# Second cross attention: one token tile and eight heads a unit, fp32r scores, five blocks of 128 keys

## The reference, cut to what matters

```python
h = _layernorm(x, ln2_w, ln2_b)
q = (h @ q_w + q_b).reshape(B, T, H, HD).transpose(0, 2, 1, 3)      # B, T, H, HD = 2, 1024, 16, 16
k = (enc @ k_w + k_b).reshape(B, S, H, HD).transpose(0, 2, 1, 3)    # S = 77, enc has 192 features
v = (enc @ v_w + v_b).reshape(B, S, H, HD).transpose(0, 2, 1, 3)
attn = jnp.einsum('bhtd,bhsd->bhts', q, k) * scale
attn = jnp.where(enc_mask[:, None, None, :], neg, attn)
attn = jax.nn.softmax(attn, axis=-1)
ca = jnp.einsum('bhts,bhsd->bhtd', attn, v).transpose(0, 2, 1, 3).reshape(B, T, C)
x = x + ca @ out_w + out_b
```

## Time and profile before

| | us |
|---|---|
| median of 3 runs | 1820.11 |
| the runs | 1815.75, 2371.29, 1820.11 |
| the profiled execution | 1816.95 |
| its span | 1815.2 |
| of it, second cross attention (1550.9 to 1678.3) | 127.4 |

### The profile page before, as it was taken

The page is one execution under the profiler, slowest core; times in us unless marked ns, Lnnn a source line. Parts: engine busy times, 40 slices in busy tenths (PEclk is TensorE's granted clock), DMA queues, the critical chain, the costliest instruction groups (busy, mean ns, idle before and its releaser), DMA issues. The chain is left out here.

```text
span 1815.2 us, 28598 instructions
## 1 busy us (share of the span) xinstructions
PE 1657.3 (91%) x9572; PEld 1025.1 (56%) x9572; DVE 1149.9 (63%) x2009; ACT 1067.1 (59%) x1407; POOL 959.6 (53%) x734
## 2 busy tenths in 40 slices
PE   5889999999999999988999889997898988898799
PEld 3334444444444444376666778885444436565579
DVE  4456777776777777385777753346778754776513
ACT  3436888888888888844554533311576763444452
POOL 1236888888888888951222630201334443466405
PEclk9999999999999999999999999997899999999899
DMA  2001211101110111030000010102333321000101
GB/s 91 18 24 36 68 41 48 41 35 41 38 61 35 41 35 36 24 105 27 1 1 1 13 33 24 30 13 49 91 72 96 81 63 42 9 1 1 35 16 47
DMA packets 54161, 70.82 MB, mean 39 GB/s; under 512 B 18160, under 2 KB 41868, under 8 KB 54063
## 3 DMA queue, kind: packets, MB, share of 16 engines
q1 hardware_dynamic: 54063, 69.54, 13.7%
HBM read 41.72 MB, written 2.37 MB: 24 GB/s over the span
## 5 line engine op out<-in xcount | busy, mean ns | idle before, releaser
L1412 POOL TENSOR_TENSOR x<-x,sa_p_buf 128x1024 f32<-128x1024 f32 x190 | 452.2, 2380 | 109.6 <-ACT sa_p_buf L1233 97.2
L1325 DVE TENSOR_REDUCE sa_mx<-sa_front 128x1 f32<-128x512 f32 x512 | 327.5, 681 | 109.1 <-PE sa_front L1126 107.7
L1233 ACT ACTIVATE sa_p_buf<-sa_score 128x1024 f32<-128x1024 f32 x256 | 249.2, 1024 | 115.9 <-PE sa_score L1164 115.9
L1179 PE MATMUL sa_out<-sa_p_buf,sa_v_buf 128*64 128x512 f32 x1024 | 246.2, 602 | 0.0
L607 ACT ACTIVATE sa_p_buf<-sa_score 128x1024 f32<-128x1024 f32 (+1 forms) x160 | 140.6, 943 | 75.0 <-PE sa_score L555 74.9
L402 DVE TENSOR_REDUCE sa_mx<-sa_front 128x1 f32<-128x512 f32 (+1 forms) x224 | 136.5, 651 | 31.4 <-PE sa_front L316 28.0
L2005 POOL TENSOR_TENSOR x<-x,bias_out 128x1024 f32<-128x1024 f32 x24 | 59.6, 2496 | 166.3 <-POOLq L2335 143.3
L1872 POOL TENSOR_TENSOR ca_probs<-ca_s_sb,ca_inv 128x616 f32<-128x616 f32 x64 | 77.9, 1218 | 120.8 <-DVE ca_inv L1787 120.8
L1179 PEld LDWEIGHTS sa_out<-sa_p_buf,sa_v_buf 128*64 128x64 f32 x1024 | 64.9, 136 | 126.9 <-issue 99.1
L1126 PE MATMUL sa_front<-sa_k_hi,sa_q_hi 64*128 64x512 f32 x512 | 116.7, 452 | 19.1 <-DVE sa_mx L1325 15.6
L1243 ACT ACTIVATE sa_score<-sa_m_all 128x1024 f32<-128x1024 f32 x128 | 130.8, 1033 | 1.0 <-DMA sa_m_all<-sa_m_line 0.6
(11 more groups left out here) (241 smaller groups left out, 3482.1 us busy)
## 6 DMA issues: line engine op xcount, KB each, us to landing
sa_v_buf<-o SPq DMA_DIRECT2D x16, 512.0 KB, 5.1
sa_m_all<-sa_m_line SPq DMA_DIRECT2D x16, 512.0 KB, 3.7
x<-sa_m_line SPq DMA_DIRECT2D x16, 512.0 KB, 4.4
x<-in_x SPq DMA_DIRECT2D x8, 512.0 KB, 6.7
sa_q_stack<-sa_hi SPq DMA_DIRECT2D x32, 128.0 KB, 2.6
sa_k_stack<-sa_hi SPq DMA_DIRECT2D x32, 128.0 KB, 2.6
sa_recip<-sa_den_out SPq DMA_DIRECT2D x32, 128.0 KB, 2.7
ff_w<-in_L_xattn_ff_w SPq DMA_DIRECT2D x16, 128.0 KB, 2.2
```

The source lines that it names most:

```text
L1179: mm = pe.matmul(out_ps[64 * j:64 * j + 64, :], v_buf[:, b, kt, 64 * j:64 * j + 64], p_buf[:, s % NPB, j, :], start=(kt == 0), stop=(kt == ...
L1233: nc.scalar.activation(p_buf[:, s % NPB], score_ps[s % len(score_ps)][:], ACT.Exp, scale=SCALE).then_inc(exp_done, G)
L1325: dve.tensor_reduce(mx[:, b, j, qt, half:half + 1], front_ps[bank(item, j)][:], AX.X, ALU.max).then_inc(drained, 1)
L1412: nc.gpsimd.tensor_tensor(acc[:, h], prev, cur, ALU.add).then_inc(added, 1)
```

## The change

A new function `block_attention` takes the place of `cross_attention` for the second block. The first cross attention keeps the old function. In the new one:

- A unit is one tile of 128 tokens and eight heads (one group): 4 chunks, 2 groups, 4 tiles, 32 units. It again has 8 by 77 = 616 scores on a partition.
- Queries and keys are split into an fp32r high part and an fp32r rest. `score` is three products (high by high, high by low, low by high), each two fp32r matmuls of 308 columns: six matmuls. The split query takes one more DVE instruction for four units (`query_low`). The masked keys exist twice: the high ones are made on DVE (`high_keys`), the low ones on POOL (`low_keys`), one each for the four combinations of group and batch.
- The 616 probabilities of a token stand without gaps (padded to 640) and are turned as five blocks of 128 keys: five transposes, an eviction of 640 numbers.
- The values stand in the same order: block by block of 128 key rows, in which a row holds the 16 features of its own head and zeros elsewhere (`v_blk`, ten blocks, made from the context repeated eight times, `ctx_rep`, and a mask `v_own`). `weighted` runs for two units at once: five float32 matmuls of 256 columns, all 128 output partitions.
- The value bias is added on ACT when a chunk's output is stored (`store`, 512 numbers, every fourth slot); DVE's `copy` is gone. `bv` is loaded as two columns in place of a broadcast row.
- POOL clears `ctx_rep` (2,560 numbers a partition) first, then makes `own`, `v_own` (640 numbers: one memset and two selects), clears `probs` (1,280), makes the low keys of the first combination; then the slots begin.

The core of the diff:

```diff
+                def score(n):
+                    i, g, b = n // TQ, group(n), batch(n)
+                    if tile(n) == 0:
+                        pe.wait_ge(q_split, i + 1)
+                        pe.wait_ge(high_set, keys_needed(n))
+                        pe.wait_ge(low_set, keys_needed(n))
+                    if n >= 2:
+                        pe.wait_ge(s_taken, n - 1)
+                    rows = slice(tile(n) * P, (tile(n) + 1) * P)
+                    for part, (qs, ks) in enumerate(((q_hi, keys_hi), (q_hi, keys_lo), (q_lo, keys_hi))):
+                        for h in range(2):
+                            mm = pe.matmul(s_ps[n % 2][:, h, 0:HH * TC], qs[:, i % 2, rows],
+                                           ks[:, g, b, h * HH * TC:(h + 1) * HH * TC], start=(part == 0), stop=(part == 2))
+                def weighted(n):
+                    if not unit(n) or n % PAIR != PAIR - 1:
+                        return
+                    pe.wait_ge(t_done, n + 1)
+                    ...
+                    for blk in range(NBLK):
+                        mm = pe.matmul(o_ps[:, first * P:(tile(n) + 1) * P], v_blk[:, batch(n), blk, group(n), :],
+                                       turned[:, n // PAIR % 2, blk].rearrange("p u t -> p (u t)"),
+                                       start=(blk == 0), stop=(blk == NBLK - 1))
+                def turn(n):
+                    pe.wait_ge(scaled, n + 1)
+                    if n:
+                        pe.wait_ge(t_done, n)
+                    else:
+                        pe.wait_ge(v_set, NV)
+                    for blk in range(NBLK):
+                        mm = pe.transpose(t_cols[:, at], probs[:, n % 2, at], ident[:])
+                def slot(n):                      # PE
+                    score(n)
+                    query(n + Q_AHEAD)
+                    for i in values_in(n):        # blocks 0-3 in slot 0, 4-6 in slot 1, 7-9 in slot 2
+                        values_of(i)
+                    weighted(n - O_LAG)
+                    turn(n - T_LAG)
+                def slot(n):                      # ACT
+                    store(n - C_LAG)
+                    exponent(n - 1)
+                    query(n + Q_AHEAD)
+                    evict(n - T_LAG)
+                def slot(n):                      # DVE
+                    take(n)
+                    query_low(n + Q_AHEAD)
+                    for i in values_in(n):
+                        values_of(i)
+                    if 0 < n < len(MADE):
+                        high_keys(*MADE[n])
+                    invert(n - 1)
+                pool.memset(ctx_rep[:], 0.0).then_inc(padded, 1)
+                own_rows(own[:], own_made, [[-dh, HR]], 0, dh, 1)
+                own_rows(v_own[:], v_own_made, [[P, NBLK], [-TC, HR], [0, dh]], 0, TC, 1)
+                pool.memset(probs[:], 0.0).then_inc(padded, 1)
+                pool.wait_ge(padded, 2)
+                low_keys(*MADE[0])
+                def slot(n):                      # POOL
+                    scale(n - D_LAG)
+                    shift(n)
+                    if n + 1 < len(MADE):
+                        low_keys(*MADE[n + 1])
-                            (bv[:], row(L1["v_b"]).to_broadcast((P, D)), kv_in[1]),
+                            (bv[:], L1["v_b"].rearrange("(g p) -> p g", p=P), kv_in[1]),
-                cross_attention(nc, "ca1", thin, hT, ctxT, ident, kv,
-                                {"key_low": lambda b: ctx_low[:, b, :]},
-                                oT, loads)
+                block_attention(nc, "ca1", hT, ctxT, ident, kv, lambda b: ctx_low[:, b, :], oT, loads)
```

272 lines of the change are left out of this document (271 added, 1 removed).

## The result

| | before | after |
|---|---|---|
| median of 20 runs, us | 1819.16 | 1823.28 |
| profiled span, us | 1815.2 | 1823.2 |
| second cross attention, entry to last store, us | 127.3 | 131.9 |

A forecast was written before the change was run, and what follows sets the result against it. A circuit through PE, DVE and POOL, not PE's work alone, was to bound the rounds; fill +8.0, steady part -2.9, drain -0.9 made the block 4.1 longer, 1821 us from the profiled 1816.95; 8 in 10: 1809 to 1833.

The forecast's parts named there:

- round: Steady state, four units from one tile 2 scores to the next: 13.7 us, against 14.34 before.
- low clock at the first scores: Fill: after PE idles about 4 us, a slow clock stretch at the first scores, costing 1.8 us.
- scores of unit 4 to unit 31: Steady part: 6.4 for two units, six rounds of 13.73 and 3.9, in all 92.7 us, 2.9 saved.
- The circuit: Steady round through scores, takes, shift, scale and turn: 0.99 + 2.48 + 4.15 + 0.61 + 5.5, giving 13.7 us.
- rival 1: Steady rounds: PE sets the pace after all, rounds of 12.3, 9.5 us less, 1812 in all; chance 0.22.
- PE idle ahead of tile 3's turn: Steady round: PE waits 0.9 us for POOL's `probs` before turn(3).
- The fill: Block start: first scores 4.1 us late behind `low_keys`, scores of unit 4 19.4 later, 8.0 later than before.
- the 6.4: Start of the steady part: time for the first two units from scores of unit 4, 6.4 us.
- Rival 3: Fill or ordered queues cost more, each weighted sum delayed by 1: 8 to 12 us, 1831 in all; chance 0.12.
- Rival 2: Block start: the fill costs little, clock full and POOL's selects cheap, 1818 in all; chance 0.1.
- Transfers: Ahead of the block: `bv` in two columns costs nothing, hidden under `project_norm`; some 3 us without that cover.
- Rival 4: Steady rounds: PE's waits make the clock fall repeatedly, slower by over 2%, up to 1904; chance 0.03.

The follow-up runs named there:

- e8: New kernel with five unused float32 matmuls of 512 columns filling PE's pause ahead of the first scores; 1.0017 of the kernel before.
- e11: New kernel with the weighted sum of tiles 0 and 1 over one key block, not five (outputs wrong there); round 13.53, block 133.69 us, one run.
- e12: New kernel with the weighted sum of tiles 2 and 3 over one key block, not five (outputs wrong there); round 12.94, block 129.00 us, one run.
- e1: New kernel with POOL clearing only the padding of the repeated context and probabilities, not all of both; 0.9995 of the kernel before.
- e5: New kernel with the fp32r split undone: plain float32 scores, query and keys kept once; 1.0005 of the kernel before.
- e9: New kernel with plain float32 scores, query three slots ahead, only padding cleared, batch 0's context repeated earlier, value blocks awaiting their own batch; 0.9969 of the kernel before.
- e4: New kernel with `query_low` moved behind `invert` in DVE's order; 1.0023 of the kernel before.
- e2: New kernel with the query made three slots ahead of its first scores, not two; 1.002 of the kernel before.
- e3: New kernel with `weighted` run for one unit at a time in every slot, not two units in every other; 0.9991 of the kernel before.
- e6: New kernel with the query three slots ahead and `query_low` two slots ahead of use; 1.0026 of the kernel before.
- e10: New kernel with the query three slots ahead, `query_low` two slots ahead and placed behind `invert`; 1.0003 of the kernel before.

## Why the prediction was right

The mechanism held: a circuit through four engines, and not PE's work, set the round, and a longer fill ate what the shorter rounds gave. That the block came within 0.5 is in part luck: scores of unit 4 came 1.5 later than forecast, and from there to unit 31 it took 1.0 less.

| step | forecast | measured |
|---|---|---|
| entry to first scores | 7.4 | 8.16 |
| first scores to scores of unit 4 | 19.4 | 20.14 |
| of it, low clock at the first scores | 1.8 | 1.2 (18.90 in e8 without it); 0.59 from 1562.8 to 1567 |
| round | 13.73 | 13.52 |
| scores of unit 4 to unit 31 | 92.7 | 91.7 |
| scores of unit 31 to the end | 11.9 | 11.94 |
| block | 131.4 | 131.94 |

- **The circuit** was the step that mattered. Counting PE's work alone would have given a round of 12.3 and a gain (rival 1, 1812); e11 and e12 show that the work alone was not the bound, and the four stages of the circuit came out at 5.27, 1.14 + 2.48, 4.11 and 0.52 where I had 5.5, 0.99 + 2.48, 4.15 and 0.61. The sum was closer than its parts: scores to take was 0.15 longer, the query slot 0.23 shorter.
- **PE idle ahead of tile 3's turn**: 0.84 for 0.9, named by the trace as a wait for `probs`.
- **The fill** was sized short by 1.5, half of it ahead of the first scores: the selects took 1.05 and 1.01 for 640 numbers, where I continued two short ones to 0.72 and so the preparation to 7.4 (my upper bound had covered it). The other half lies behind them: PE waited 1.27 ahead of turn(0) and 2.04 ahead of turn(1), where my layout had 0.6 and about 1.7. Without the low clock this part took 18.9 (e8), where mine comes to 17.6; the slow stretch, put at 1.8, cost 1.2 and hid half of that.
- **A low stretch I had not counted**: the second, at 1583. The way from scores(4) to scores(6) took 6.81 for 6.4; in e1 and e8, with a full clock there, it took 5.82 and 5.83. So the 6.4 was 0.6 too long by itself, and the stretch cost 1.0.
- **Rival 3** (value blocks wait, `evict` delays each weighted sum) was hardly there: the weights of tile 0's weighted sum waited 0.20 for their eviction, where it put 1 to 1.5 a round. An fp32r matmul of 308 columns took 0.14, by columns.
- **Rival 2** (cheap selects, full clock) fell with both of its conditions.
- **Transfers**: `bv` in two columns took 2.7 from issue to landing, ahead of the block, and nothing in the block waited for it, as forecast.
- **Rival 4** fell: with transposes, scores and waits of up to 0.84 us the granted clock was 1.00 from 1590 to 1670. It was 1.00 in e12 too, where PE paused for 1.75 in each round (windows of e12):

```profile
1590.00:1670.00 80.00, 64.75 (x368) 51.10 (x369) 64.77 (x106) 41.45 (x63) 60.02 (x50) 1.00 0.00 1
```

  The window that I held against it, 1674 to 1677 in the kernel before, was a weak argument: 1.5 us behind its end a low stretch begins (granted 0.75 from 1677 to 1680, 0.68 from 1680 to 1683).
- What the Trainium skill (TensorE: Matmul & The Clock Gate, Part 4: PE-mode transpose) says of transposes and the clock, that they do not count as busy in the same way, did not become visible in a steady round: the granted clock was 1.00 there, with twenty transposes in each round.

## What to carry to other kernels

Less work on the busiest engine is worth only what the circuits leave: follow one round from start to start through every engine's queue and double buffer, with the transfers in program order, and compare its length with the busy time. Work that comes in lumps, such as a product for two units at once beside a query, lengthens a circuit at constant work, and a helper instruction placed early in another engine's order (here `query_low`) costs nothing in one arrangement and 0.4 us a round in the next. A leaner loop with a long preparation in front of it has to pay for that from few rounds: here seven rounds of 0.8 did not pay for a fill that was 10 us longer.

## What the runs showed of the hardware

The granted clock at the block's edges is not the same from one execution to the next. At the entry the first query ran at full clock (1.88) in the traces of before, after, e5, e9 and e12 and took 3.1 to 3.6 in the nine others (3.35 in e1), with nearly the same code ahead of it; in the drain it was full in after and low in e8 (0.67) and e11 (0.52 from 1680 to 1687). Such a stretch moved the block by 1.7 in e8 and 2.5 in e11 (13.30 from take(31) to the end), as much as several of the edits above; the round, at full clock, repeated to 0.01 (13.52, 13.52, 13.52, 13.53 and 13.53 in after, e4, e8, e1 and e11), and is what the verdicts rest on.

A pause of PE alone does not tell whether a low stretch follows. In nine traces PE paused for 2.4 us or more ahead of its first scores or its first turn (before, after, e2, e3, e4, e6, e10, e11, e12), and in each the clock was low when it went on or within 1.5 us; in e8, which filled the pause, it was full there. But in e1 it was low behind pauses of only 0.93 and 1.17, and the stretch at 1583 in the new kernel stands behind pauses of 1.27 and 2.04, which e1 and e8 had as well (1.28 and 2.05) with a full clock behind them.
